# The last block's messages in an order of their own, over freed PSUM banks, with the additions at the end

## What is computed

```python
Wh = h @ W + b
sim = dot(Wh[row], Wh[col]) / max(|Wh[row]| * |Wh[col]|, EPS)
base = adj_v * softplus(deg_coeff[0] * deg_v + deg_coeff[1]) * (row != col)
prop_pos = segment_sum((base * relu(sim))[:, None] * Wh[col], row)
prop_neg = segment_sum((base * -relu(-sim))[:, None] * Wh[col], row)
out = scale * (coeff[0] * prop_pos + coeff[1] * prop_neg + coeff[2] * Wh)
```

## Time and profile before

| | before |
|---|---|
| median of 3 runs | 1021.93 us (1019.66 to 1024.82) |
| the profiled execution's own time | 1016.11 us |
| its span | 1014.4 us |
| TensorE (PE) busy | 843.9 us, 83% |
| VectorE (DVE) busy | 857.1 us, 84% |
| ScalarE (ACT) busy | 616.6 us, 61% |
| GpSimd (POOL) busy | 191.9 us, 19% |
| mean granted TensorE clock | 0.935 |

### The profile page before, as it was taken

One profiled execution on the slowest core, in us unless ns is written; L12 is line 12 of the kernel. 1 busy time (PEld: TensorE's weight loads), 2 busy tenths in 40 slices (PEclk: granted clock), 3 DMA queues, 4 the chain that ended last, 5 costly groups with the idle time before them and its releaser, 6 DMA issues. The chain is left out here.

```text
span 1014.4 us, 33668 instructions
## 1 busy us (share of the span) xinstructions
PE 843.9 (83%) x14240; PEld 591.0 (58%) x14240; DVE 857.1 (84%) x1214; ACT 616.6 (61%) x2090; POOL 191.9 (19%) x364
## 2 busy tenths in 40 slices
PE   0596449998888988888889889529999998999996
PEld 0362335555555555555555555219999998885553
DVE  8987869999999999899999999465666896786996
ACT  0764438788777877677878877249999912111000
POOL 4824722223222322122222221000000000000000
PEclk9888559999999999999999999759999999997999
DMA  8943215766766677557765776589200000964893
GB/s 200 234 148 85 55 48 136 176 150 172 170 169 147 175 167 179 136 145 179 178 157 150 187 175 147 131 314 414 91 2 2 2 1 23 373 256 159 334 399 112
DMA packets 44698, 164.33 MB, mean 162 GB/s; under 512 B 14244, under 2 KB 16374, under 8 KB 40822
## 3 DMA queue, kind: packets, MB, share of 16 engines
q1 hardware_dynamic: 33990, 133.22, 42.6%
q0 software_dynamic: 8288, 27.59, 13.4%
q10 hardware_dynamic: 2256, 1.23, 0.5%
HBM read 78.63 MB, written 63.72 MB: 140 GB/s over the span
## 5 line engine op out<-in xcount | busy, mean ns | idle before, releaser
L1171 PEld LDWEIGHTS b_ps<-b_mv,b_soh 64*128 64x128 bf16 x9600 | 162.8, 95 | 136.7 <-DVE b_mv L1056 65.2
L1171 PE MATMUL b_ps<-b_mv,b_soh 64*128 64x50 bf16 (+1 forms) x9600 | 187.6, 189 | 65.8 <-DVE b_mv L1056 36.6
L1391 PE MATMUL layers_ps<-layers_u,layers_c 128*128 128x192 bf16 x2500 | 211.5, 248 | 12.6 <-ACT layers_u L1573 10.0
L1391 PEld LDWEIGHTS layers_ps<-layers_u,layers_c 128*128 128x128 bf16 x2500 | 208.5, 99 | 17.8 <-DVE layers_y L1697 8.0
L946 ACT ACTIVATE b_c_row<-b_ps 128x300 bf16<-128x300 f32 (+1 forms) x275 | 117.0, 426 | 57.8 <-PE b_ps L1171 49.5
L1056 DVE TENSOR_TENSOR b_mv<-b_mv,b_parts 128x2808 bf16<-128x2808 bf16 x100 | 145.9, 1459 | 1.6
L964 ACT ACTIVATE b_pos<-b_ps,k_coef 128x1024 f32<-128x1024 f32 x100 | 92.9, 929 | 70.5 <-PE b_ps L1171 70.2
L1582 ACT ACTIVATE k_passed<-layers_c 128x128 bf16<-128x128 bf16 x450 | 131.4, 293 | 0.0
L1094 DVE TENSOR_TENSOR b_y<-b_sim,b_ps 128x512 f32<-128x512 f32 (+1 forms) x175 | 109.7, 627 | 24.5 <-PE b_ps L1225 17.1
L1051 DVE TENSOR_TENSOR b_soh<-k_numbers,b_bits 128x2304 bf16<-128x2304 bf16 x100 | 122.2, 1222 | 0.0
L1083 DVE SCALAR_TENSOR_TENSOR b_sim<-b_ps,k_coef,b_pos 128x1024 f32<-128x1024 f32 x100 | 104.3, 1043 | 6.9 <-ACT b_pos L964 6.9
(11 more groups left out here) (275 smaller groups left out, 1095.1 us busy)
## 6 DMA issues: line engine op xcount, KB each, us to landing
layers_c<-g_blocks SPq DMA_DIRECT2D x25, 1600.0 KB, 9.2
g_blocks<-b_g_row SPq DMA_DIRECT2D x52, 400.0 KB
c_blocks<-b_c_row SPq DMA_DIRECT2D x25, 800.0 KB
g_blocks<-head_odd SPq DMA_DIRECT2D x48, 400.0 KB
layers_c<-c_blocks SPq DMA_DIRECT2D x12, 1600.0 KB, 26.3
k_passed<-b_sent POOLq DMA_DIRECT2D x24, 768.0 KB, 7.0
prep_attr<-in_edge_attr SPq DMA_DIRECT2D x2, 1883.0 KB
prep_attr<-in_edge_attr SPq DMA_DIRECT2D x1, 1876.0 KB
```

Of the source, the lines that this page charges most:

```text
L1171: return nc.tensor.matmul(out, lhsT, rhs, start=start, stop=True, skip_group_check=True)
L1391: return nc.tensor.matmul(out_, lhsT, rhs, start=start, stop=True, skip_group_check=True)
```

## The change

The last block's message gets orders of its own, END on TensorE and VEND on VectorE. As no lot is in flight any more, its groups use the banks of the lots: similarities of group 0 to 3 in banks 4-5, 0-1, 2-3 and 4; turned chunks in banks 6 and 7 in turn; propagated sums in banks 5, 0, 2 and 1. TensorE waits once at the start of `end` for the last evacuation and the last `send`, and for less after that: `turn` i for y i-2 and no longer y i-1, `propagate` for no addition, `sims` for no `similar` except in group 3. ScalarE's `positive` takes over the wait that keeps the one tile `pos` from being overwritten. The four additions stand last. SyncE waits for `summed` before it stores the last block's counts, and so before all five of that block's stores.

```diff
+END = [("sims", 0), ("turn", 0), ("turn", 1), ("sims", 1), ("sims", 2), ("turn", 2), ("turn", 3), ("prop", 0), ("prop", 1),
+       ("sims", 3), ("turn", 4), ("turn", 5), ("prop", 2), ("prop", 3), ("turn", 6), ("prop", 4), ("prop", 5), ("prop", 6)]
+VEND = [("sim", 0), ("y", 0), ("y", 1), ("sim", 1), ("y", 2), ("y", 3), ("sim", 2), ("y", 4), ("y", 5), ("sim", 3), ("y", 6),
+        ("add", 0), ("add", 1), ("add", 2), ("add", 3)]
...
+        ENDSIM, ENDPROP = [SIM, 0, 2, SIM], [SIM + 1, 0, 2, 1]
...
+        closing = lambda v: isinstance(v, int) and v == NB - 1
...
+                if b == NB - 1:
+                    sp.wait_ge(s["summed"], 32 * BYSUM)
                 counts_out(b)
...
+                if closing(v):
+                    act.wait_ge(s["sgn"], NG * v + (g + 1))
...
-                pe.wait_ge(s["sgn"], NG * v + (g + 1))
+                if not closing(v):
+                    pe.wait_ge(s["sgn"], NG * v + (g + 1))
+                elif g == 3:
+                    pe.wait_ge(s["sgn"], NG * v + 2)
...
-                pe.wait_ge(s["scaled"], NC * v + (i + 1))
+                pe.wait_ge(s["scaled"], NC * v + (i if closing(v) and i else i + 1))
...
-                pe.wait_ge(s["added"], NG * v + (g + 1 if g < NG - 1 else 1))
                 bank, low = PR if g < NG - 1 else AT, F * (i % 2)
+                if closing(v):
+                    bank = ENDPROP[g]
+                else:
+                    pe.wait_ge(s["added"], NG * v + (g + 1 if g < NG - 1 else 1))
...
+                last = r * NB + (NB - 1)
+                if not again(r):
+                    pe.wait_ge(s["evac"], 3 * NL * last + (3 * NL + 6))
+                    pe.wait_ge(s["added"], NG * last + 1)
+                for what, i in ORDER if again(r) else END:
```

More of the change, by code:

```diff
@@ L727, in build @@
                                 else tile[:, 0:wide(g)])
-        both = lambda g: ps[:, SIM:SIM + 2, :] if wide(g) == 1024 else ps[:, SIM, 0:wide(g)]
+        both = lambda g, at=SIM: ps[:, at:at + 2, :] if wide(g) == 1024 else ps[:, at, 0:wide(g)]
+        closing = lambda v: isinstance(v, int) and v == NB - 1
+        read = lambda v, g: both(g, ENDSIM[g]) if closing(v) else both(g)
         again = lambda r: not isinstance(r, int)
@@ L963, in positive @@
                 act.wait_ge(s["sims"], NG * v + (NG + g + 1))
-                nc.scalar.activation(side(pos, g), both(g), ACT.Relu, scale=coef[:, 0:1]).then_inc(s["pos"], 1)
+                if closing(v):
+                    act.wait_ge(s["sgn"], NG * v + (g + 1))
+                nc.scalar.activation(side(pos, g), read(v, g), ACT.Relu, scale=coef[:, 0:1]).then_inc(s["pos"], 1)
             def send(v, g):
@@ L1082, in similar @@
                 dve.wait_ge(s["pos"], NG * v + (g + 1))
-                nc.vector.scalar_tensor_tensor(side(sim[g % 2], g), both(g), coef[:, 1:2], side(pos, g),
+                nc.vector.scalar_tensor_tensor(side(sim[g % 2], g), read(v, g), coef[:, 1:2], side(pos, g),
                                                ALU.mult, ALU.add).then_inc(s["sgn"], 1)
@@ L1093, in weigh @@
                 if isinstance(v, int):
-                    nc.vector.tensor_tensor(y[g % 2][:, here], sim[g % 2][:, here], ps[:, AT, 0:n], ALU.mult).then_inc(s["scaled"], 1)
+                    nc.vector.tensor_tensor(y[g % 2][:, here], sim[g % 2][:, here], ps[:, AT + i % 2 if closing(v) else AT, 0:n],
+                                            ALU.mult).then_inc(s["scaled"], 1)
                 else:
@@ L1148, in end @@
             def end(r):
-                for what, i in VORDER:
+                for what, i in VORDER if again(r) else VEND:
                     weighing(r * NB + (NB - 1), NB - 1, what, i)
@@ L1214, in sims @@
                     by = unit if isinstance(v, int) else whT
-                    ins = mm(ps[:, SIM + i % 2, 0:P * nh], wh_b[par][rows, :], by[rows, P * h0:P * (h0 + nh)], True)
+                    ins = mm(ps[:, (ENDSIM[g] if closing(v) else SIM) + i % 2, 0:P * nh], wh_b[par][rows, :], by[rows, P * h0:P * (h0 + nh)], True)
                 ins.then_inc(s["sims"], 1)
@@ L1224, in turn @@
                 for j in range(nh):
-                    ins = nc.tensor.transpose(ps[:, AT, P * j:P * j + P], a_row[par][:, h0 + j, :], k["ident"][:])
+                    ins = nc.tensor.transpose(ps[:, AT + i % 2 if closing(v) else AT, P * j:P * j + P], a_row[par][:, h0 + j, :], k["ident"][:])
                 ins.then_inc(s["at"], 1)
@@ L1265, in end @@
             def end(r):
-                for what, i in ORDER:
+                last = r * NB + (NB - 1)
[3 more added lines that the diff above has]
+                for what, i in ORDER if again(r) else END:
                     if what == "sims":
-                        sims(r * NB + (NB - 1), 0, i)
+                        sims(last, 0, i)
                     if what == "turn":
-                        turn(r * NB + (NB - 1), 0, i)
+                        turn(last, 0, i)
                     if what == "prop":
-                        propagate(r * NB + (NB - 1), 0, i)
+                        propagate(last, 0, i)
             for name, n in (("lot", NL), ("sims", NG), ("at", 2 * NC), ("propped", 2 * NC + 1)):
```

## The result

The changed kernel took 1009.67 us (median of 4 runs, 1005.57 to 1015.59) against 1022.12 (4 runs, 1019.66 to 1024.82): ratio 0.9895, 95% interval 0.9862 to 0.9928. The profiled execution took 1007.57 us, its span is 1005.9. Ratios and means here leave out executions more than 1.5% above the fastest of the same kernel: 5 of 103 of the kernel before, none of the others.

What follows compares the result with a forecast made beforehand. The prediction took the last message's late landing to bound the end of `build`, and the stores after the change. `layers` would begin at 655.0, not 661.4: 1021.93 - 6.4 = 1015.5 us, range 1013.0 to 1020.0.

Steps and rivals of the forecast that it cites:

- message's first packets: End of `build`: with an empty queue, the last message's packets begin 1.8 us after issue, bounds 1.5 and 2.45.
- both parts landed: End of `build`: the last message's large and small parts land 5.7 us after its first packet, at 643.4.
- stores, from landing to landing: End of `build`: from the message's landing to that of the last block's counts and gate stores, 11.2 us (10.6 to 12.5).
- SyncE's exit: End of `build`: from SyncE's arrival at the barrier to the others' first instruction, 0.4 us, bounds 0.2 and 2.67.
- gain in the stretch: From the last message's issue to the first matmul of `layers`: `layers` begins at 655.0 instead of 661.4, 6.4 us earlier.
- the median of the three runs shown: Whole kernel before: 1021.93 us, 5.8 above its profiled execution, the starting value from which the gain was subtracted.
- a fixed chain: From the barrier before `layers` on: everything that follows, SyncE's loads of the counts included, shifts by the same 6.4 us.
- rival C: End of `build`: the last message is slow by itself, not through the stores; 1.3 us slower, 1023.2 us; chance 0.06.
- D: End of `build`: TensorE's clock falls inside the new order, so no gain, 1021.4 us; chance 0.05.
- A: End of `build`: the stores are faster and the compute engines bound; gain 8.6, 1013.3 us; chance 0.07.
- B: End of `build`: the exit past the loop is delayed, with DMA queues full of stores; gain 4.1 to 5.1; chance 0.17.
- the late landing: End of `build`: the 24th message lands at 648.8, behind the g stores, and holds back VectorE's first addition.

Runs made afterwards that it cites:

- the wait alone: Kernel before with its old order, plus only SyncE's wait for `summed` before the last block's counts store; ratio 0.9937 (0.9902 to 0.9973) to the kernel before.
- the order alone: Changed kernel without SyncE's wait, so the last block's stores start at once; ratio to the kernel before 0.9942, and 0.9912 when run again.

## Why the prediction was right or wrong

**Mechanism: right.** Each step against the profile, in us after the issue of the last message:

| step | predicted | measured |
|---|---|---|
| message's first packets | 1.8 | 1.4 |
| both parts landed | 7.5 | 6.5 |
| stores, from landing to landing | 11.2 | 11.7 |
| stores landed | 18.7 | 18.2 |
| SyncE's exit | 0.4 | 0.5 |
| first `similar` | 2.3 | 2.2 |
| additions begin, end | 11.2, 13.6 | 10.6, 12.7 |
| first matmul of `layers` | 19.1 | 18.75; 18.64, 18.50, 18.90 in the other profiles |
| gain in the stretch | 6.4 | 6.9 (25.65 - 18.70, means of 3 and 4 profiles) |

The landing came 1.0 us early, inside its bounds: with nothing ahead the packets begin 1.4 us after the issue, just less than the lower bound of 1.5, and from there to the landing they take 5.0 us instead of 5.7. VectorE ran 0.9 us faster than reckoned: two "y" in a row take 1.28 us and not 1.38, the four additions 2.06 and not 2.4. Neither decides, as the stores come last.

**Where it failed: the step from the profiled execution to a median, and the range.** The forecast was 1021.93 - 6.4 = 1015.5, and its range was drawn from the bounds of the stretch alone. The first term, "the median of the three runs shown", was taken as fixed. The runs of before, 98 over all groups, have a mean of 1018.2 us and a standard deviation of 4.0, from 1010.1 to 1027.4: the term was 3.7 us high. The second term, the gain, measured 6.9, 0.5 more. With both set right the sum is 1011.3, and the changed kernel's 30 runs have a mean of 1009.8 (standard deviation 3.4). The last 1.5 us lie in what the prediction put at nothing, all that is outside the stretch ("a fixed chain"). Even 1009.8 is below the range, so the miss is not the luck of four executions; that the first comparison showed a gain of 10.7 us and not one near 8.4 is. A median of four such runs is uncertain by some 2.5 us by itself, and separate loads of the kernel before stood 2.9 us apart on one chip (1015.0 and 1017.9). The statement that 0.5% is what a measurement tells from no change was too bold for the same reason. Two slips decide nothing: by the prediction's own terms rival C's thresholds are 647.5 and 649.8, not 647.2 and 649.5, and D's sum gives 660.5, not 660.9.

**What the whole gain is.** All runs taken together, the changed kernel is 8.4 us faster (standard error 0.7, taken as if all runs were independent, which they are not). Of this 6.9 lie in the stretch. The mean low-clock time of its runs is 122.6 us against 135.2. The 60 us from the last message on hold 34.1, 37.5 and 41.0 us of it in the three profiles of before and 27.3, 30.7, 27.3 and 30.7 in the four of the changed kernel: 8.5 us less, since TensorE no longer works its way through the end of `build` at the lower level. The remaining 4.1 us at 0.38 are 1.6 us, and 6.9 + 1.6 = 8.5. These last 1.6 look like chance, though it is not proved. The four other kernels with the new order and all stores (43 runs) are 7.4 us faster than before, and their stretches say 7.3. Other totals miss their stretch by more, and both ways: the wait alone gained 6.4 us with 3.8 in the stretch, the kernel without gate stores 6.1 with 10.0. And the last message is issued at 637.0 us on average in the ten profiles with the new order, at 636.4 in the three of before, so nothing ahead of it is faster.

**The rivals.** *A*, compute engines bound: refuted by SyncE's waits and by the run without gate stores. Its premise, a faster message, holds for the start only: the message still moved at 197 to 221 GB/s (below). By the Trainium skill's fit for such a DMA (DMA: Bandwidth & Descriptors, "Anatomy of one DMA — SWDGE (gpsimd) path") the estimate is 3.8 us; with nothing beside it the large part took 5.8. *B*, a dearer exit: there, but hidden. With the order alone, stores still in flight when VectorE was done, the exit took 4.1 and 4.2 us, with quiet queues 3.0 to 3.4; with the wait alone, whose stores had landed 0.8 us before VectorE was done, it took 3.7, so not all of the difference need come from the queues. That fits what the Trainium skill says of branches that must fetch their target by DMA (Runtime: NRT & Kernel Launch, "Instruction fetch mechanics"), and the packets of the instruction queue do come later beside the stores (14.7 to 17.0 us, without them 10.6 to 12.9); how much of an exit hangs on them no run shows. *C* is refuted: the message was slow because of the stores. *D* too: the clock stayed at 1.00 in the new order,

```profile
634.00:649.00 15.00, 10.11 (x53) 4.62 (x49) 10.11 (x15) 3.71 (x4) 1.46 (x2) 1.00 0.81 199
```

and fell only when TensorE had nothing left to do. What the prediction did not see is that the order alone would bring as much as both. It named the late landing as the bound and shortened it, but with the additions last the late landing costs VectorE only 1.77 us.

## What to carry to other kernels

When something waits for a transfer, first move the wait behind all work that doesn't need it: here that brought 7.0 us of stretch, and making the transfer earlier then added nothing, because it made the stores late, and they then bound. Put a gain that was worked out from one profile against runs whose own scatter you know, and compare landmarks inside the profile: a stretch between two events repeated within 0.4 us where whole runs scattered over 17. If totals move without a reason, look at TensorE's granted clock before you look for a cause in the change, and at TensorE's pauses of 1 to 3 us: here the clock fell behind them, in one execution and not in the next.

## What was not expected of the hardware

The two DMA queues did not share the engines evenly. With nothing queued, the message's first packets came 1.4 us after its issue. With the counts' store issued 0.4 us ahead they came 2.5 to 2.6 us after it. With the four gate stores behind the counts as well they came at 4.4 us in the three profiles of before (the prediction, from slots of half a microsecond, read 4.6), but at 2.6 in the two of the order alone, which has the same stores: there SyncE's four issues took 3.7 and 3.4 us instead of 5.3, and the second came later (1.0 and 1.4 us after the message's issue instead of 0.5). With two gate parts ahead of the wait it was 4.5 us, with one 2.6. So the message waits longer when two gate stores are issued before its packets are ready; what rule decides it no run shows. The accumulating message moves at half the rate of the counts' store even alone. Stretches of the changed kernel, the message alone and then the counts alone:

```profile
635.00:638.50 3.50, 3.07 (x19) 1.54 (x16) 2.51 (x4) 1.91 (x2) 0.46 (x1) 1.00 1.02 202
641.00:643.00 2.00, 1.87 (x11) 0.66 (x9) 1.91 (x3) 0.37 (x1) 0.00 (x0) 1.00 1.03 410
```
